# Expert layer with one list of rows per expert in place of every expert over every token

## The reference

```python
xn = layernorm(x)                                  # 4096 tokens x 256
score = sigmoid(xn @ gate_w.T)                     # 16 experts
top = the 4 largest of score + gate_b              # per token
w = score[top] / sum(score[top]) * 2.5
for e in range(16):                                # only tokens that chose e have w > 0
    gate, up = split(xn @ w13[e].T, 2)             # 128 columns each
    y += w_e * (silu(gate) * up) @ w2[e].T
y += shared expert (all tokens, weight 1)
out = x + layernorm(y)
```

## Time and profile before

| | us |
|---|---|
| median of 3 runs (2584.97 to 2589.25) | 2587.27 |
| the profiled execution, its own time | 2582.47 |
| its span, first to last instruction | 2580.7 |
| PE busy | 2159.6 |
| DVE busy | 1637.6 |
| ACT busy | 840.8 |
| POOL busy | 607.1 |
| the expert layer's first DMA issued at | 1843.82 |

### The profile page before, as it was taken

One profiled execution on the slowest core, in us unless ns is written; L12 is line 12 of the kernel. 1 busy time (PEld: TensorE's weight loads), 2 busy tenths in 40 slices (PEclk: granted clock), 3 DMA queues, 4 the chain that ended last, 5 costly groups with the idle time before them and its releaser, 6 DMA issues. The chain is left out here.

```text
span 2580.7 us, 31081 instructions
## 1 busy us (share of the span) xinstructions
PE 2159.6 (84%) x11049; PEld 1341.9 (52%) x11152; DVE 1637.6 (63%) x2846; ACT 840.8 (33%) x1530; POOL 607.1 (24%) x357
## 2 busy tenths in 40 slices
PE   0878987997997897888898798855279999999998
PEld 0544544554554454554454455422157777777775
DVE  3235796696696597588679669658355555555553
ACT  0342442352343333434344235310133222222222
POOL 0000242243143043133224214314111120112010
PEclk9779999899898998999999989875589999999999
DMA  4000000000000000000000000000210000000000
GB/s 121 1 1 9 1 1 18 1 2 17 1 1 9 10 1 9 10 1 1 18 1 1 18 1 1 1 8 0 65 55 19 17 17 17 0 17 16 16 1 17
DMA packets 32303, 33.46 MB, mean 13 GB/s; under 512 B 4496, under 2 KB 31184, under 8 KB 31952
## 3 DMA queue, kind: packets, MB, share of 16 engines
q1 hardware_dynamic: 32144, 31.38, 4.0%
HBM read 22.99 MB, written 8.39 MB: 12 GB/s over the span
## 5 line engine op out<-in xcount | busy, mean ns | idle before, releaser
L557 DVE TENSOR_TENSOR_SCAN s_buf<-r_work,kvb 128x512 f32<-128x512 f32 x256 | 366.3, 1431 | 0.0
L655 POOL TENSOR_TENSOR p_buf<-s_buf,r_work 128x512 f32<-128x512 f32 x128 | 151.7, 1185 | 486.7 <-DVE s_buf L557 486.7
L1563 PE MATMUL mbank<-m_xh,w_hi 128*128 128x512 f32 x544 | 228.7, 420 | 0.0
L1371 DVE TENSOR_TENSOR hl<-hf,hh 128x512 fp32r<-128x512 f32 x136 | 93.9, 691 | 199.8 <-ACT hh L1478 199.2
L710 ACT ACTIVATE probs<-bank_s,nmx 128x256 f32<-128x256 f32 (+1 forms) x512 | 186.5, 450 | 103.4 <-DVE nmx L420 99.8
L655 POOL TENSOR_TENSOR r_work<-s_buf,r_work 128x512 f32<-128x512 f32 x128 | 164.9, 1288 | 234.8 <-DVE s_buf L557 234.8
L1563 PE MATMUL mbank<-m_xl,w_hi 128*128 128x512 f32 x544 | 215.5, 396 | 0.0
L1563 PE MATMUL mbank<-m_xh,w_lo 128*128 128x512 f32 x544 | 215.5, 396 | 0.0
L728 ACT ACTIVATE pt<-bank_s 128x1024 f32<-128x1024 f32 (+1 forms) x128 | 117.5, 918 | 240.7 <-PE bank_s L988 240.7
L1474 ACT ACTIVATE sg<-mbank 128x512 f32<-128x512 f32 x136 | 81.2, 597 | 325.7 <-PE mbank L1563 325.6
L546 DVE TENSOR_TENSOR kvb<-r_work,bank 128x512 f32<-128x512 f32 x256 | 174.2, 681 | 16.2 <-PE bank L1106 5.4
(11 more groups left out here) (251 smaller groups left out, 4231.4 us busy)
## 6 DMA issues: line engine op xcount, KB each, us to landing
w_raw<-in_w SPq DMA_DIRECT2D x17, 256.0 KB, 2.8
x_new<-in_x SPq DMA_DIRECT2D x8, 512.0 KB, 3.5
x_after_rwkv<-x_b SPq DMA_DIRECT2D x8, 512.0 KB, 3.5
m_x_tok<-x_after_rwkv SPq DMA_DIRECT2D x8, 512.0 KB, 3.8
out<-m_x_tok SPq DMA_DIRECT2D x8, 512.0 KB, 2.9
w_raw<-in_w2e SPq DMA_DIRECT2D x17, 128.0 KB, 2.7
work<-in_w SPq DMA_DIRECT2D x2, 1024.0 KB
wrk<-in_wrk SPq DMA_DIRECT2D x1, 1024.0 KB
```

Source lines behind the costliest of these rows:

```text
L557: V.tensor_tensor_scan(s_buf[:, n % 2, 1:S + 1], dec[:, n // HD, :], kvb[:, n % 2, :], 0.0, ALU.mult, ALU.add).then_inc(sem["state"], 1)
L655: G.tensor_tensor(p_slot(n), s_buf[:, n % 2, 0:S], rf[:, n // HD, :], ALU.mult).then_inc(sem["rs"], 1)
L1563: ins = T.matmul(o, w[:, e, cols:cols + P], m, start=first and c == 0, stop=last and c == 2)
```

## The change

The layer works in three stages, and two DRAM tensors are added, `x_rows` (16 regions of 4096 rows of 1152 bytes, one region per expert) and `y_rows` (four rows of 1024 bytes for each token).

- Ahead of its work in `mid_token_layers`, ACT issues 17 DMAs that write an empty row into every row of `x_rows`. GpSimd makes the empty row. ACT waits for them at the end of the first part.
- Stage A, per batch: normalise and route as before (the exponential is now ACT's), the shared expert alone over 512 tokens, its result kept in SBUF. DVE and PE count the rows chosen so far for each expert (`count_rows`, `place_rows`), which gives each of a token's four choices a row in `x_rows`. GpSimd issues 16 indirect DMAs of 128 rows each: normalised token, 16 routing weights, 16 result row numbers. The 16 experts' weights are split meanwhile, two per batch.
- Between: DVE and PE make a table of 144 tiles, each with its expert, its 128 rows and the offset of its weights; short lists are filled up with empty rows.
- Stage B, 144 tiles in 18 groups of eight: SP loads a tile; PE turns it, multiplies gate and up with the expert's weights at an address read from the table into registers, turns the hidden values, multiplies down; DVE applies weight and up (`weighted`), ACT and DVE split into high and low and copy the result to one of four buffers; GpSimd scatters the 128 result rows to `y_rows` with one indirect DMA.
- Stage C, per batch: four results per token and the token's input are loaded, PE sums the four and the shared expert's result with the identity at full precision, then statistics, normalisation, sum and store.

The core of the diff:

```diff
-    mid_token_layers(nc, t, x3)
-    expert_layer(nc, t, x3, out)
+    mid_token_layers(nc, t, x3, x_rows)
+    expert_layer(nc, t, x3, x_rows, y_rows, out)
...
+            sc.wait_ge(rows_made, 1)
+            for e in range(NE):
+                sc.dma_start(x_rows[e * B * S:(e + 1) * B * S].rearrange("(r p) c -> p r c", p=P),
+                             empty_row[:].unsqueeze(1).broadcast_to([P, B * S // P, ROW])).then_inc(rows_empty, 16)
...
+                for u in range(GROUP):
+                    sp.wait_ge(sem["h_f"], at(B, "h_f", 0) + g * GROUP + u - GROUP + 1)
+                    sp.dma_start(xs[:, u, :], x_rows[bass.ds(base[u] * P, P)]).then_inc(xs_in[u // 2], 16)
...
+            for b in range(B):
+                route(b)
+                if b + 1 < B:
+                    start_stats(b + 1)
+                hidden(b)
+                place_rows(b)
+                if b + 1 < B:
+                    norm(b + 1)
+                weights_low(2 * b + 1)
+                low(b)
+                if b + 1 < B:
+                    for k in range(NK):
+                        x_low(b + 1, k)
+                weights_low(2 * b + 2)
...
+            def weighted(s, g, u, e):
+                ve.wait_ge(sem["silu"], at(B, "silu", 0) + s + 1)
+                y = u % Y_RING
+                if u >= Y_RING or not (isinstance(g, int) and g == 0):
+                    ve.wait_ge(ys_out[y], g * (16 * GROUP // Y_RING) + u // Y_RING * 16)
+                V.tensor_copy(y_idx[:, y:y + 1], xs[:, u, bass.ds(e + (D + NE), 1)].bitcast(U32))
...
+            def rows_to_experts(b):
+                gp.wait_ge(sem["routed"], at(b, "routed", 2))
+                for i in range(NT):
+                    for k in range(TOPK):
+                        G.indirect_dma_start(x_rows, bass.IndirectOffsetOnAxis(slot[:, b % 2, i, k:k + 1], 0), xr[b % 2][:, i, :], None
+                                             ).then_inc(rows_out[b % 2], 16)
...
+            for s in range(TILES):
+                rows_to_tokens(s, s // GROUP, s % GROUP)
...
+                for u in range(GROUP):
+                    s = g * GROUP + u
+                    gate_up_s(s, u, c[u + 2])
+                    if u or not first:
+                        turn_h(s - 1, (u - 1) % GROUP)
+                    turn_s(s + 2, g + (u + 2) // GROUP, (u + 2) % GROUP)
+                    if u > 1 or not first:
+                        down_s(s - 2, g - (u < 2), (u - 2) % GROUP, c[u], not first or u > 3)
```

More of the change, by code:

```diff
@@ L1274, in _ @@
+            for b in range(2):
+                load_y(b)
+            for b in range(B):
+                sp.wait_ge(sem["x_final"], b + 1)
+                sp.dma_start(rows(out[b:b + 1]), x_tok[b % 2][:]).then_inc(sem["x_out"], 16)
+                if b + 2 < B:
+                    sp.wait_ge(sem["x_out"], 16 * (b + 1))
+                    load_y(b + 2)
             sp.wait_ge(sem["x_out"], B * 16)
@@ new lines, in _ @@
+            weights_low(0)
+            norm(0)
+            for k in range(NK):
+                x_low(0, k)
+            for b in range(B):
+                route(b)
[11 more added lines that the diff above has]
+                weights_low(2 * b + 2)
@@ new lines, in group @@
+            def group(g, first):
+                e = table_row(mybir.EngineType.DVE, 0, slice(2, 2 + GROUP) if first else bass.ds(g * GROUP + 2, GROUP), NE - 1)
+                for u in range(GROUP):
+                    s = g * GROUP + u
+                    weighted(s, g, u, e[u])
+                    if u or not first:
+                        low_h(s - 1, (u - 1) % GROUP)
+                    low_x(s + 2, (u + 2) % GROUP)
+                    if u % 2 and (u > 1 or not first):
+                        y_odd(s - 2, (u - 2) % GROUP)
@@ L1421, in _ @@
+            for b in range(B):
+                end(b)
         @block.gpsimd
@@ L1449, in _ @@
+            for s in range(TILES):
+                rows_to_tokens(s, s // GROUP, s % GROUP)
+            for b in range(B):
+                root(B + b)
         @block.scalar
@@ new lines, in group @@
+            def group(g, first):
+                for u in range(GROUP):
+                    s = g * GROUP + u
+                    silu_s(s, u)
+                    if u or not first:
+                        high_h(s - 1, (u - 1) % GROUP)
+                    high_x(s + 2, (u + 2) % GROUP)
+                    if u % 2 == 0 and (u > 1 or not first):
+                        y_even(s - 2, (u - 2) % GROUP)
+            high_x(0, 0)
+            high_x(1, 1)
+            group(0, True)
+            with sc.Fori(1, N_GROUPS) as g:
+                group(g, False)
@@ L1627, in _ @@
-            batches(pe, body)
-            for e in (NX - 2, NX - 1):
-                down(B - 1, e, False)
-            for half in range(2):
-                turn_y(B - 1, half)
+            pe.wait_ge(w_split, 1)
+            for b in range(B):
+                gate_up(b)
+                count_rows(b)
+                if b + 1 < B:
+                    for k in range(NK):
+                        turn_x(b + 1, k)
+                down(b)
+                if b + 1 < B:
+                    route(b + 1)
@@ new lines, in _ @@
+            pe.wait_ge(w_split, NX)
+            pe.wait_ge(list_ready, 1)
+            pe.wait_ge(sem["y_kept"], at(B, "y_kept", 0))
+            turn_s(0, 0, 0)
+            turn_s(1, 0, 1)
+            group(0, True)
+            with pe.Fori(1, N_GROUPS) as g:
+                group(g, False)
+            c = table_row(mybir.EngineType.PE, 2, slice(TILES, TILES + 2), (NE - 1) * WE)
+            turn_h(TILES - 1, GROUP - 1)
+            for u in range(2):
+                down_s(TILES - 2 + u, N_GROUPS - 1, GROUP - 2 + u, c[u], True)
```

669 lines of the change are left out of this document (362 added, 307 removed).

## The result

The changed kernel takes 2772.55 us (median of 4 runs, 2766.71 to 2776.92) against 2586.43 us of the kernel before in the same rounds: ratio 1.0715, 95% interval 1.0695 to 1.0735. It is 7.2% slower, where 2.2% faster was forecast. Its profiled execution has a span of 2775.1 us.

A forecast was written before the change was run, and what follows sets the result against it. TensorE's matmuls were taken to bound the expert layer. Stage B starting at 2050, C at 2412 and ending at 2504, plus 20 at the start, gave 2524 of span; forecast 2530 us, range 2470 to 2590, eight in ten 2445 to 2720.

The forecast's parts named there:

- The fill: Start: writing empty rows lasts 199 to 267 us, under the first batches; DVE begins some 20 us later.
- the upper bound of 230: Start: some 230 us lost if constant loads queue behind the fill or ACT cannot issue 17 DMAs ahead.
- The first rival: Start: the fill holds up constant loads and ACT's first instruction, 230 us in place of 20, 2740 in all; chance 0.17.
- Stage A: Routing, 8 batches: GpSimd's 16 indirect DMAs at 1.2 us and a power, 20.6 us a batch, just above DVE's 19.
- The rival by which GpSimd needs 2.0 us or more each: POOL queue, 272 indirect DMAs: at 2.0 us each 2640 in all, at 3.1 near 2900; chance 0.14.
- Stage B: Expert tiles: 144 at 2.2 us plus 18 groups at 2 us, 353 us, then 9 for emptying and last landing.
- The tile: Stage B: 2.2 us per tile, a little above PE's 2.05 and the loop's 1.97; bounds 1.97 and 3.5.
- the loop itself: Stage B: `weighted` waits for the scatter four tiles earlier to land; 5.9 us for three tiles, 1.97 each.
- about one trip, 2 us a group: Stage B: reading 8 to 10 values into registers once in eight tiles costs 2 us; bounds nothing and 17.
- Stage C: Last 8 batches: first out after 18 us, 21 for each two, 92 us in all.
- TensorE's term: Stage C: ten full-precision matmuls of 512 columns at 0.45 us, 4.5 us a batch.
- The rival of TensorE's clock or the registers: Stage B: lower clock makes a tile 3.5 us, 187 us more, 2717 in all; halfway 2620; chance 0.09.

The follow-up runs named there:

- the runs with 10 and 18 values: Changed kernel with groups of eight tiles (10 values for TensorE), 2772.6 us, and with groups of 16 instead (18 values), 2787.3 us.
- the version without tests: Changed kernel plus eight result buffers, fill split around SP's loop, early stage C loads, no bounds tests, groups of 8: 2437.97 us, ratio 0.9433 to the kernel before.

## Why the prediction was wrong

Its own sum ended at 2524 us of span; the span is 2775.1. The 251 us are 166 at the start, 16 in stage A, 37 in B and 32 in C.

**The fill.** This is the step that failed: "I take 20, since the loads of before were issued without a wait for each other." The measured price is 186, near the upper bound of 230. What was dismissed was the other half of that bound, "ACT cannot issue 17 such DMAs ahead and misses its first work at 63.71 us". The argument drew on SP's loads of before, some 50 of them and 8 MB in all; the fill has transfers of 4.7 MB each, and ACT's queue held ACT until they were nearly written. Moving the issue off ACT (1862 instead of 2030 at the layer's start) and halving it (1940) both show that it is the queue of the issuing engine and not the bandwidth. The first rival named the mechanism and 230 us; it got 0.17.

The 20 us for DVE's first instruction came near the 25.6 measured, but partly by luck. The last constant that it waits for, in SP's queue before and after:

```profile
25.73 0.42 SPq L245 DMA_DIRECT2D x_tok<-in_c_lmask  x1
```

```profile
46.29 0.46 SPq L250 DMA_DIRECT2D x_tok<-in_c_lmask  x1
```

20.6 of the 25.6 us lie in SP's issuing, which was stretched while the fill stood on ACT's queue (18 of the small loads took 0.9 to 1.4 us to issue, 0.4 to 0.6 before), and only 5 in the way from the last issue to DVE's start (16.7 us, 11.7 before). So even the loads, which the argument took for free to issue, were held up. Why, by full DMA engines or by something the two queues share, no run shows. All of it lay in the shade of ACT's own delay.

This step alone doesn't make the error. With the fill's price at nothing, the changed kernel's own stages end at 1843.8 + 745.2 = 2589 us of span, 8 more than before; with the 20 us as costed at 2609, where the forecast had 2524. So the edit of the expert layer as such gained nothing either, and the forecast had a gain of 77 us there. Three terms were mis-sized, 85 us together.

**Stage A** took 222 us, 206 forecast. GpSimd's queue is the bound, as said. Its timeline, with one batch's end and the next one's beginning.

```profile
2102.19 0.96 POOL L1556 DMA_INDIRECT x_rows<-m_xr,m_slot  x1 [0.31 <-issue]
2103.17 1.04 POOL L1550 TENSOR_TENSOR m_rstd<-m_vare,m_mhalf 128x4 f32<-128x4 f32 x1
2106.96 1.04 POOL L1556 DMA_INDIRECT x_rows<-m_xr,m_slot  x1 [2.75 <-DVE m_said L1422]
2108.30 1.49 POOL L1556 DMA_INDIRECT x_rows<-m_xr,m_slot  x1 [0.30 <-issue]
2110.09 0.96 POOL L1556 DMA_INDIRECT x_rows<-m_xr,m_slot  x1 [0.30 <-issue]
```

The group of the 128 over the whole span gives the mean.

```profile
L1556 POOL DMA_INDIRECT x_rows<-m_xr,m_slot x128 | 133.1, 1040 | 50.2 <-issue 37.1 <-DVE m_said L1422 13.0
```

One indirect DMA occupies the queue for 1.04 us and 0.29 us of issue, 1.33 and not 1.2; and 13.0 us in all, 1.6 a batch, are waits for DVE's places. 16 by 1.33, 1.04 for the power and 1.6 are 23.9 us a batch, where 20.6 was forecast and 24 is seen. The routing itself began 20 us after the layer's start and not 24, which gives some back. The rival by which GpSimd needs 2.0 us or more each didn't come to pass: the longest of the 128 took 1.79 us. A smaller lengthening is there: 21 of the 128 took over 1.1 us, and each of them lies beside a subtraction of DVE that reads two operands (`w_lo`, `hl` or `xl`), as 1.66 us beside one of 0.96; over the stage it comes to 10 us. The Trainium skill ("SBUF — State Buffer", SBUF: two separate sides, The DVE blocks DMA trap) has GpSimd unable to write descriptors during a two-port operation of DVE, and some 3.1 us for a transfer beside one. The 10 us may be of that kind; 3.1 us for one no run here shows, with DVE busy half of stage A.

**Stage B** took 399 us, 362 forecast. The tile was right: (398.8 less 18 by 4.1) / 144 = 2.26 us, 2.2 forecast, and what binds it between the edges is the scatter's loop over four buffers, as said; eight buffers took 47 us off the stage. The fit has luck in it: the loop itself was costed at 1.97 us and is 0.3 dearer, and the margin of 0.2 had been put on for addresses from registers. Wrong was "about one trip, 2 us a group" for the registers: 4.1 us. By the runs with 10 and 18 values it is no trip for the group but 0.36 us for each value on TensorE and 0.5 on DVE, and most of TensorE's is the test of its bounds, since an edge falls to 1.4 us without it. 18 by 2.1 us are 38, the whole error of the stage. The Trainium skill ("Runtime: NRT & Kernel Launch", Instruction fetch mechanics) gives some 200 ns for each register that the runtime's own instruction loads from HBM, which is another load than this one from SBUF, and no run here shows it. Beside it stand 0.14 us a value without tests (1.4/10) and 0.36 with them.

**Stage C** took 124 us, 92 forecast. TensorE's term was half of what it is. The code has ten matmuls of 512 columns a batch, the records 20.

```profile
2717.92 5.54 PE L1805 MATMUL mbank<-w_lo,m_ident 128*128 128x512 f32 x8 [9.24 <-DMA m_x_tok<-x_after_rwkv]
2723.30 1.02 PE L1806 MATMUL mbank<-y_sh,m_ident 128*128 128x512 f32 x2
2724.15 3.60 PE L1805 MATMUL mbank<-w_lo,m_ident 128*128 128x512 f32 x8
```

Each full-precision matmul as written stands there twice, at 0.45 us each (3.60/8): 9 us a batch and not 4.5. The row that the 0.45 came from counts records too: its 16 are eight written matmuls. It was taken for the price of a written one. The router's 16 records are eight written matmuls in the same way; nothing in the sum hangs on that. Load, sum, end and store of two batches stand in a row, 29 us and not 21.

**The rival of TensorE's clock or the registers** came to pass in small: the clock was 0.84 over stage B, where 0.72 was feared, and the tile stayed at 2.26 us; the registers did stretch the stage, by 38 us, where the rival's 187 stood for the clock. What the clock cost can't be read off: in the version without tests the matmuls were busy 28 us less at 0.96, in the one with the tests alone taken off, at 0.93, they took 148 ns each against 154 in the changed kernel (266.26/1732).

## What to carry to other kernels

Several large transfers in a row are no "fire and forget": one of 4.7 MB alone let its engine go at once, but each further one held it until those ahead were largely written. So ask for each engine what is queued behind its issues, and put bulk writes where a queue has nothing else to do. Values that steer a loop from a list are paid for one by one and on every engine that reads them, and a run-time test can be most of that price; take it off all readers at once, or little moves (14 us from one reader, 77 from all). When several limits lie just under each other (ring, edges, clock), cost the pair and not only the one on top: in stage B eight buffers alone brought 47 us, the tests alone 35, and both together, with stage B's matmuls also less long busy, 122.

## What the runs showed of the hardware

- An ACT or SP queue with several transfers of 4.7 MB (4096 pieces of 1152 bytes each) lets its engine go only at the pace of the writing, 14.5 us a transfer at 325 GB/s; the last issue alone, a small one, stood 14 us. A single one was issued in 0.5 to 1.8 us, two in 12. The loads of before, of 1 MB at most, never showed it.
- While ACT's queue was full of them, 18 of SP's small loads took 0.9 to 1.4 us each to issue instead of 0.4 to 0.6.
- Reading ten values from SBUF into TensorE's registers took 4.1 us with bounds tests and about 1.4 without; 16 on DVE took 8.0 with them; eight on SP took 2.1 us less without them.
- A scatter of 128 rows by an indirect DMA took GpSimd 0.96 us at the least, and 1.26 us from one to the next; beside a subtraction of DVE with two operands up to 1.79.
- The same 1732 matmuls were busy 266, 255 and 228 us with a granted clock of 0.84, 0.83 and 0.96 and stages of 399, 354 and 278 us. The clock rose when the edges were closed, also where the stage stayed at 364 us (0.93).
- One or two transfers of the fill inside SP's loop made a batch of the first part 2 us longer than in the kernel before and 3 to 5 longer than in the changed kernels that have none there, the same for one as for two; why was not found.
